# Regrouping the dense stages of the first network in a four-network graph kernel

## What is computed

```
h = relu(layernorm(x))
for l in (0, 1):
    p = segment_sum(h[dst], src) + h          # pooling over the sources, with a self loop
    p = p / degree
    y = relu(batchnorm(p @ W0 + b0, mg, mb))   # statistics over the 6250 nodes
    h = relu(batchnorm(y @ W1 + b1, g, b))
x = x + h
h = relu(layernorm(x))                         # over the 128 features: input of the second network
```

## Time and profile before

| what | value |
|---|---|
| median of the three runs | 3235.7 us |
| profiled execution, span from first to last instruction | 3240.8 us |
| PE matmul busy | 2943.5 us, 91% of the span |
| PE weight load / DVE / ACT / POOL busy | 1740.9 / 1047.2 / 729.8 / 1114.7 us |
| mean granted TensorE clock | 0.951 of full |

### The profile page before, as it was taken

One profiled execution on the slowest core, in us unless ns is written; L12 is line 12 of the kernel. 1 busy time (PEld: TensorE's weight loads), 2 busy tenths in 40 slices (PEclk: granted clock), 3 DMA queues, 4 the chain that ended last, 5 costly groups with the idle time before them and its releaser, 6 DMA issues. The chain is left out here.

```text
span 3240.8 us, 44117 instructions
## 1 busy us (share of the span) xinstructions
PE 2943.5 (91%) x18657; PEld 1740.9 (54%) x18657; DVE 1047.2 (32%) x1860; ACT 729.8 (23%) x1173; POOL 1114.7 (34%) x1012
## 2 busy tenths in 40 slices
PE   1799969997899869999999999999899877999998
PEld 1688835553444335555555555554355664555554
DVE  5899922223200261211111111113311483222122
ACT  4799912223100230000000000001100383011000
POOL 5000013330000004562562663664167101553564
PEclk6899979998999979999999999999899987999999
DMA  7133599994466226666665665664566213665665
GB/s 260 50 129 129 163 244 173 164 170 89 120 147 146 44 66 206 178 171 169 177 175 165 182 178 163 173 173 121 146 181 179 78 54 101 176 180 161 171 170 156
DMA packets 768367, 492.61 MB, mean 152 GB/s; under 512 B 362500, under 2 KB 749836, under 8 KB 767568
## 3 DMA queue, kind: packets, MB, share of 16 engines
q1 hardware_dynamic: 705362, 395.76, 50.5%
q0 software_dynamic: 30112, 62.69, 6.6%
q10 hardware_dynamic: 32702, 31.44, 3.1%
HBM read 334.89 MB, written 76.82 MB: 127 GB/s over the span
## 5 line engine op out<-in xcount | busy, mean ns | idle before, releaser
L2159 PE MATMUL acc<-tbuf,hs 128*128 128x448 fp8e4 x8232 | 1602.0, 354 | 20.0 <-PEq L1242 8.8
L2136 POOL DMA_INDIRECT grow<-hrows,glist x882 | 940.6, 1066 | 791.9 <-PE acc L2183 388.3
L2159 PEld LDWEIGHTS acc<-tbuf,hs 128*128 128x128 f16 x8232 | 801.2, 98 | 762.9 <-issue 52.5
L2298 DVE TENSOR_TENSOR edge_loc<-iota,gdl 128x768 f16<-128x768 bf16 x147 | 140.6, 971 | 743.9 <-PE acc L2183 714.4
L731 PE MATMUL quad<-K,S 128*128 128x196 bf16 x1568 | 278.0, 250 | 17.6 <-DVE K L655 17.6
L1627 PE MATMUL acc<-tbuf,hs 128*128 128x512 fp8e4 (+1 forms) x1300 | 279.6, 369 | 14.9 <-DMA tbuf<-table 14.9
L711 ACT ACTIVATE stage<-quad 128x784 fp8e4<-128x784 f32 x392 | 287.4, 838 | 11.6 <-PE quad L731 5.8
L735 PE MATMUL deg<-K,S 128*128 128x196 bf16 x1568 | 276.8, 248 | 0.0
L1500 PE MATMUL acc<-tbuf,hs 128*128 128x512 fp8e4 (+1 forms) x1300 | 267.4, 369 | 0.7 <-issue 0.7
L2267 ACT ACTIVATE H<-B,vectors 128x448 f32<-128x448 f32 (+2 forms) x56 | 37.4, 668 | 820.3 <-DVE B L2338 820.3
L1500 PEld LDWEIGHTS acc<-tbuf,hs 128*128 128x128 f16 x1300 | 123.6, 98 | 144.4 <-issue 4.3
(11 more groups left out here) (301 smaller groups left out, 2008.5 us busy)
## 6 DMA issues: line engine op xcount, KB each, us to landing
tbuf<-table SPq DMA_DIRECT2D x294, 448.0 KB, 3.6
tbuf<-table SPq DMA_DIRECT2D x294, 336.0 KB, 3.2
table<-stage SPq DMA_DIRECT2D x6, 5488.0 KB, 19.4
grow<-hrows,glist POOLq DMA_INDIRECT x882
hrows<-hs SPq DMA_DIRECT2D x28, 448.0 KB, 4.4
feat<-in_edge_attr_dram ACTq DMA_DIRECT2D x27, 448.0 KB, 6.6
C<-factors ACTq DMA_DIRECT2D x2, 3136.0 KB, 12.5
table<-stage SPq DMA_DIRECT2D x2, 2744.0 KB, 12.2
```

What stands on the lines that cost most here:

```text
L2136: g.indirect_dma_start(out=grow[:, n % 2, t, :], out_offset=None, in_=k.hrows[l % 2], in_offset=bass.IndirectOffsetOnAxis(k.glist[:, i // ...
L2159: mm = T.matmul(acc(s, h), rows[l % 2][:, g * US + r, part, :], counts[:, (r - lo) * STRIP + h * HALF:(r - lo) * STRIP + (h + 1) * HALF], ...
L2298: V.tensor_tensor(hot[:, n % 2, :, :], k.iota[:, 0:P].unsqueeze(1).to_broadcast([P, GH, P]), k.gdl[:, i // GU, i % GU * GH:(i % GU + 1) * ...
```

## The change

For the path without spills:

- `pool_with_features` gets `after=(W0, b0)`. After tile step 3 (`UP_AT`) of group g PE multiplies group g-1 of B by W0 in one 512-column product into banks 4 and 5 (`up`), and at step 4 DVE takes it out with the bias, back into B, and takes its `bn_stats` (`up_leaves`). The last group follows at the end.
- `dense_and_pool` is one stage for the rest of layer 0 and for the pooling of layer 1. It takes the batch norm's constants on small steps of DVE and ACT, and normalises with one ACT instruction per group (scale and bias per partition, relu) instead of one of DVE and one of ACT. PE follows with the product by W1 over four banks; ACT takes out the odd groups, DVE the even ones and all `bn_stats`. Then constants again, ACT normalises H by groups, PE transposes each group, ACT and DVE write `hs`, and PE does the matmuls of group 0 of the pooling as the blocks of `hs` come. Groups 1 to 12 follow, with layer 1's product by W0 (`up`) in the middle of each. SP loads the table from the start of the stage. `target_factors` comes behind the splitting on DVE.
- `dense_and_norm` is one stage for the rest of layer 1, the residual, the layer norm and the split with the second network's weight. The residual's addition goes from DVE to POOL (behind the seven indirect DMAs), chunks are 512 nodes, the two waves hold 7 and 6 groups, the inverse of wave 0 is put on DVE behind the 11th centring and that of wave 1 behind the third scaling, and scaling, turning, high and low part run behind one another group by group.
- `k.parts`, `k.middle` and `k.rstd` are 512 wide; the last two are allocated after the first pooling.

```diff
@@ pool_with_features, tensor
+                def up(g):
+                    pe.wait_ge(acc_read.h, acc_read.at(g + 1))
+                    if g >= 2:
+                        pe.wait_ge(up_out.h, up_out.at(g - 1))
+                    T.matmul(k.bank[4 + g % 2][:, 0:width(g) * P], after[0], dst[:, group_at(g)], start=True, stop=True
+                             ).then_inc(up_ok.h, 1)
...
+                        if after and g and s == UP_AT:
+                            up(g - 1)
                         for u in batches(g * NU + s):
                             features(u)
+                if after:
+                    up(LAST_G)
@@ Dense
+    def first_scalar(self, act):
+        k = self.k
+        self.roots(act, 0)
+        for i in range(NSG + 2):
+            if i < NSG:
+                self.normal(k.B, i).then_inc(self.y.h, 1)
+            g = i - 2
+            if g >= 0 and g % 2:
+                act.wait_ge(self.sum.h, self.sum.at(g + 1))
+                k.nc.scalar.activation(k.H[:, group_at(g)], self.bank(g), ACT.Identity, bias=self.bias
+                                       ).then_inc(self.out[1].h, 1)
...
@@ dense_and_pool, tensor
+            layer.products(pe)
+            for b in range(4):
+                pe.wait_ge(a_in[b].h, a_in[b].at(16))
+            for c in range(NSG + 1):
+                if c < NSG:
+                    turn(c)
+                if c:
+                    pe.wait_ge(lo_ok.h, lo_ok.at(c))
+                    sources(0, tiles(c - 1))
+            pe.wait_ge(deg_step.h, deg_step.at(1))
...
+                sources(g, range(0, NL // 2))
+                up(g - 1)
+                sources(g, range(NL // 2, NL))
+            up(LAST_G)
@@ dense_and_norm, vector
+            layer.first_vector(dve)
+            for g in range(NSG):
+                centre(g)
+                if g == W0 + 3:
+                    inverses(0)
+            third(0)
+            for g in range(NSG + 1):
+                if g < NSG:
+                    finish(g)
+                if g == 2:
+                    inverses(1)
+                if g:
+                    low(g - 1)
+                if g == 3:
+                    third(1)
@@ network
-            dense(0, tbuf)
-            split_rows(k, H, False, 1, None, None, tbuf, False)
-            pool_sources(k, B, tbuf, 1)
+            if spilled:
+                dense(0, tbuf)
+                split_rows(k, H, False, 1, None, None, tbuf, False)
+                pool_sources(k, B, tbuf, 1)
+            else:
+                dense_and_pool(k, W["a1"], (vec(1), vec(2), vec(3), vec(4), vec(5)), (W["b0"], vec(6)), tbuf)
```

More of the change, by code:

```diff
@@ L1018, in _ @@
                 dve.wait_ge(middle.h, middle.at(w + 1))
-                V.tensor_tensor(k.parts[64:64 + WCH, w, :], root, k.middle[0:WCH, w, :], ALU.subtract
+                V.tensor_tensor(k.parts[64:64 + WCH, w, 0:CH], root, k.middle[0:WCH, w, 0:CH], ALU.subtract
                                 ).then_inc(inverse.h, 1)
@@ L1060, in layer_norm, with product @@
               ln_spread=NCH, ln_final=NCH, ln_added=NCH if add else 0)
-def product(k, terms, dst, func, bias, stats=False, tbuf=None, group=0, sums=False, lists=False):
+def product(k, terms, dst, func, bias, stats=False, tbuf=None, group=0):
     nc = k.nc
@@ new lines, with __init__, bank, wait_out @@
+class Dense:
+    def __init__(self, k, weight, gain0, shift0, bias, gain1, shift1):
+        self.k, self.weight, self.bias = k, weight, bias
+        self.norms = ((gain0, shift0), (gain1, shift1))
+        self.stat, self.root, self.const = k.sem("d_stat"), k.sem("d_root"), k.sem("d_const")
+        self.y, self.sum = k.sem("d_y"), k.sem("d_sum")
+        self.out = [k.sem("d_out0"), k.sem("d_out1")]
+        self.chain, self.links = k.sem("d_chain"), 0
+    def bank(self, g):
+        return self.k.bank[2 + g % 4][:, 0:width(g) * P]
+    def wait_out(self, eng, g):
+        eng.wait_ge(self.out[g % 2].h, self.out[g % 2].at(g // 2 + 1))
+    def link(self, dve, ins):
+        self.links += 1
+        ins.then_inc(self.chain.h, 1)
+        dve.wait_ge(self.chain.h, self.chain.at(self.links))
+    def products(self, pe):
+        k = self.k
+        for g in range(NSG):
+            pe.wait_ge(self.y.h, self.y.at(g + 1))
+            if g >= 4:
+                self.wait_out(pe, g - 4)
+            k.nc.tensor.matmul(self.bank(g), self.weight, k.B[:, group_at(g)], start=True, stop=True
+                               ).then_inc(self.sum.h, 1)
+    def constants(self, dve, n):
+        V, mv, (gain, shift) = self.k.nc.vector, self.k.bn_mv, self.norms[n]
+        V.bn_aggr(mv[:, 0:2], self.k.bn_stats[:, 0:NSG, :].rearrange("p a b -> p (a b)")).then_inc(self.stat.h, 1)
+        dve.wait_ge(self.root.h, self.root.at(n + 1))
+        self.link(dve, V.reciprocal(mv[:, 3:4], mv[:, 2:3]))
+        self.link(dve, V.tensor_tensor(mv[:, 4:5], mv[:, 3:4], gain, ALU.mult))
+        self.link(dve, V.scalar_tensor_tensor(mv[:, 5:6], mv[:, 0:1], -1.0, mv[:, 4:5], ALU.mult, ALU.mult))
+        V.tensor_tensor(mv[:, 5:6], mv[:, 5:6], shift, ALU.add).then_inc(self.const.h, 1)
+    def roots(self, act, n):
+        mv = self.k.bn_mv
+        act.wait_ge(self.stat.h, self.stat.at(n + 1))
+        self.k.nc.scalar.activation(mv[:, 2:3], mv[:, 1:2], ACT.Sqrt, bias=self.k.eps[:, 0:1]).then_inc(self.root.h, 1)
+        act.wait_ge(self.const.h, self.const.at(n + 1))
+    def normal(self, v, g):
+        mv = self.k.bn_mv
+        return self.k.nc.scalar.activation(v[:, group_at(g)], v[:, group_at(g)], ACT.Relu, scale=mv[:, 4:5],
+                                           bias=mv[:, 5:6])
+    def first_scalar(self, act):
+        k = self.k
+        self.roots(act, 0)
[7 more added lines that the diff above has]
+                                       ).then_inc(self.out[1].h, 1)
+    def first_vector(self, dve):
+        k, V = self.k, self.k.nc.vector
+        self.constants(dve, 0)
+        for g in range(NSG):
+            if g % 2 == 0:
+                dve.wait_ge(self.sum.h, self.sum.at(g + 1))
+                V.tensor_scalar(k.H[:, group_at(g)], self.bank(g), self.bias, None, ALU.add).then_inc(self.out[0].h, 1)
+            self.wait_out(dve, g)
+            found = V.bn_stats(k.bn_stats[:, g, :], k.H[:, group_valid(g)])
+        self.link(dve, found)
+        self.constants(dve, 1)
+    def over(self):
+        self.k.advance(d_stat=2, d_root=2, d_const=2, d_y=NSG, d_sum=NSG, d_out0=(NSG + 1) // 2, d_out1=NSG // 2,
+                       d_chain=self.links)
@@ L2751, in program @@
         k.spread = sb("spread", [3 * 32, NCH, D], BF16)
-        k.parts = sb("parts", [3 * 32, 2, CH], BF16)
-        k.middle = sb("middle", [NCH, 2, CH], BF16)
+        k.parts = sb("parts", [3 * 32, 2, 512], BF16)
         k.zero = sb("zero", [P, 1], F32)
@@ L2828, in network @@
             prepare(k, tbuf)
-            pool_with_features(k, k.B, tbuf, w["edge_attr_32"])
+            pool_with_features(k, k.B, tbuf, w["edge_attr_32"], None if spilled else (k.W["a0"], k.vec(0)))
+        k.middle = ctx.enter_context(nc.sbuf_tensor(f"middle{k.next()}", [NCH, 2, 512], BF16))
+        k.rstd = ctx.enter_context(nc.sbuf_tensor(f"rstd{k.next()}", [NCH, 2, 512], F32))
         k.A, k.H = (big(n) for n in "AH")
@@ L2839, in dense @@
             v0 = 6 * l
-            product(k, [(W["ab"[l] + "0"], B)], B, ACT.Identity, vec(v0), stats=True, tbuf=first_buffer,
-                    sums=(l == 0 and not spilled), lists=(l == 1 and not spilled))
+            product(k, [(W["ab"[l] + "0"], B)], B, ACT.Identity, vec(v0), stats=True, tbuf=first_buffer)
             batch_norm_relu(k, B, vec(v0 + 1), vec(v0 + 2))
```

346 lines of the change are left out of this document (320 added, 26 removed).

## The result

| | before | changed |
|---|---|---|
| median of four runs | 3236.5 us (3234.7 to 3244.9) | **3191.5 us** (3189.6 to 3193.3) |
| ratio, 95% interval | | 0.9861 (0.9848 to 0.9874) |
| span of the profiled execution | 3240.8 us | 3189.3 us |
| mean granted clock | 0.951 | 0.959 |

Faster by 45.0 us of median, 1.4%; forecast were 45 us less, and a time of 3191. The page of the changed kernel (compare): PE is busy for 13.6 us less in a span that is 51.5 shorter, since most of what goes is idle time.

The account below looks back on a forecast made before the run. PE bounds the full poolings, so time is to be had only where PE stands still or runs at half clock. Layer 0's 28 us and layer 1's 18 make 46, taken as 45: 3191 us, range 3174 to 3213.

Parts of the forecast that it names:

- Step 1: Products by W0 move into both poolings: 10.3 us per layer on PE, DVE's share hidden, 1.3 us behind the last group.
- The third rival: In both poolings PE waits for DVE's 1.4 us at each of 24 W0 products: 34 us given back, 3225; 6%.
- Steps 2 and 3: Batch norm constants 1.7 us, four times, barrier 0.6 per merged program; product by W1 17.4 us per layer, ACT the bound.
- Step 4: Layer 0's normalising, turning and splitting merged with the second pooling's group 0 matmuls, PE the bound: 33.5 us.
- Step 5: Layer 1's residual and norm: PE's mean and variance at 2 x 0.86 us per group, 28.4 us in all.
- Step 6: Layer 1's scaling, turning and splitting: a latency chain of 1.67 us per group, 31.2 us with inverse and half clock.
- Half clock in both programs: In both merged programs PE never gets past clock 0.50: 63 us lost against 45, 3254 us; 4%.
- for turning alone: Transposes in layer 0's stretch with group 0 do not count towards full clock: its 28 us lost, 3219 us; 4%.
- W0 not hidden: The third rival: DVE's 1.4 us per W0 product holds up PE in both poolings, 34 us given back, 3225; 6%.
- Full clock at once: In the merged stages the half-clock terms of steps 3 to 6 fall away: 12 us more saved, 3179 us; 8%.

Follow-up runs that it names:

- the version with four more steps: Changed kernel plus low parts two scalings later, unread products before each W1 product and at the second wave's inverse, later wait for the second pooling's tables; 3185.7 us.

## Why the prediction was right

That the forecast of 45 us was met to 0.1 is luck in part. By the trace layer 0 gives 29.2 us (28 forecast) and layer 1 19.0 (18 forecast), and the second network starts 47.4 us earlier in one profile and 49.9 in the other, where the first pooling ends 2.0 us earlier; the median moved by 45.0. What follows is on the mechanism.

**What bounds** (right). The poolings are full of PE work, the gaps are idle or at half clock; the gain came out of the gaps, since PE's busy time fell by no more than 13.6 us of the 51.5.

**Step 1** (right for the whole, wrong in one place). The products cost 10.4 and 10.7 on the path and are hidden on DVE, as the kernels with the products behind the poolings and with three statistics show. The third rival's cover is thin: two more `bn_stats` per group use it up in places. I had not priced what the move alone is worth; the 6.7 us that I derived later carried layer 0's 3.07 us of wait at the barrier into layer 1.

**Steps 2 and 3** (the sum right, two sizes in it off). Constants 1.65. With the clock held up, constants and product take 16.5 us in both layers (the version with four more steps: 771.56 to 788.03, 1077.88 to 1094.37), in the changed kernel 19.1 and 18.1. So half clock at the start costs 2.6 and 1.6, where 1.5 was charged, and the product at full clock 14.8, where I had 16. The two errors cancel, which is luck; in the other profiles with the same code the two steps take 17.9 to 19.2 us in layer 0 and 18.0 to 19.1 in layer 1.

**Step 4** (right, 0.9 too long). PE is without a pause from 797 us to the end of group 0. The clock is at 0.50 up to 801 and at 1.00 from 803 on, and the kernel with the turning first shows 9 us of merging gain. The Trainium skill (TensorE: Matmul & The Clock Gate, Part 4: PE-mode transpose) has it that transposes do not engage the full clock. With source matmuls between them the stretch is at 1.00; in the kernel with the turning first, with short pauses, at 0.50. The trace of before, with transposes alone at 1.00, still speaks against it as a general rule.

**Step 5** (mechanism right, a size off). 30.1 us instead of 28.4. "2 x 0.86" was taken from products that share their weights. Where mean and variance alternate, each costs 1.00. The kernel before had told it in its own norm, where PE's timeline reads

```profile
1161.08 0.92 PE L960 MATMUL acc<-B,gather 128*7 128x448 f32 x2
1161.93 1.02 PE L954 MATMUL acc<-A,avg 128*128 128x448 f32 x2
1162.88 0.92 PE L960 MATMUL acc<-B,gather 128*7 128x448 f32 x2
```

That is 1.80 us for two products of 448 columns, and 1.50 by the earlier trace rows. In the changed kernel the weights change at each product from 1110.61 to 1128.07 us, some 18 times, which makes 2.6 us more. The half clock lasted from 1104.8 to some 1109.2 us there, a loss of 2.2 where 3 were charged, and PE's pause at the first wave's inverse was 1.25 where 1.5 were.

**Step 6** (right, 2.0 too long). 1.66 us per group, 1.67 forecast; the chain of latencies is confirmed by breaking it. The 2.0 lie in the first pass and the half clock: 29.2 less 20.3 for the groups and 5.1 for inverse and third part leave 3.8, where 1.5 and 4 were charged. "The merging of scaling and split itself brings little": 0.6 us of trace, nothing in time.

**Rivals.** Half clock in both programs, and for turning alone: refuted by 24 us at 1.00 with PE full. W0 not hidden: refuted, though its margin is thin. Full clock at once: did not happen; keeping PE busy on purpose gave it ahead of both products by W1 (of use in layer 0, and in the version with four more steps in both) and, with the low parts later, through the whole second wave, but not ahead of the turning.

## What to carry to other kernels

Price a merged stage by its slowest engine and its start at half clock, and a moved product by its full length where PE is full: the gain is in pauses and barriers, not in PE work. Take a matmul's duration from rows where it alternates with the neighbour that it will have, since only these hold the 0.15 us that a change of weights cost here. When a stage gets shorter, look at once for the load that was just in time for it.

## What was not expected of the hardware

- Behind the second wave's inverse PE's clock was at 0.50 after a pause of 1.4 us as after one of 4.3 us, and filling the pause ahead of the turning but for its last 2.5 us did not keep the clock. Only with the pause of 4.3 us filled and the low parts later did it stay at 1.00 through the second wave.
- Two float32 products of 512 columns take 2.01 us where the weights change at each, and 1.86 where they change at every second one.
- One stage with unchanged code (the third network's node update) differs by 5 us, 200.8 to 205.9, from execution to execution; a difference of that size between two spans says nothing of an edit elsewhere.
- The product by W1 with its constants, unchanged code too, took 17.9 to 19.2 us in layer 0, so 1 us between two traces says nothing either.
- What stays open: why the differences in time are not those of the traces. Some are smaller (9.3 against 12.6, 5.8 against 8.1, 16 against 19.4), some larger (6.4 against 2.7 with PE kept busy, 5.7 against 3.2 with the low part later). Each trace is one execution, and the node update's scatter is as large.
